# Cross-attention on one Trainium2 core: scores in three PSUM banks instead of two, and the turning and placing of the row maxima one slot later each

## The reference

```
q = x @ Wq + 2 * (x @ Aq @ Bq)          # 256 x 1024
k = c @ Wk + 2 * (c @ Ak @ Bk)          # 256 x 256
v = c @ Wv + 2 * (c @ Av @ Bv)
scores = q_head @ k_head.T / sqrt(32)   # per head 256 x 256
attn   = softmax(scores)
out    = x + context @ Wo + 2 * (context @ Ao @ Bo)
```

## Time and profile before

| | |
|---|---|
| time, median of 3 runs | 685.08 us (685.04, 685.08, 685.62) |
| the profiled execution's own time | 685.43 us |
| its span, first to last instruction | 683.2 us |
| busy: PE, PEld, DVE, ACT, POOL | 666.6, 527.1, 518.6, 468.5, 368.4 us |
| mean granted TensorE clock | 0.997 |
| attention loop, first to last scores (L1490) | 45.4 to 525.0 us |

### The profile page before, as it was taken

The page is one execution under the profiler, slowest core; times in us unless marked ns, Lnnn a source line. Parts: engine busy times, 40 slices in busy tenths (PEclk is TensorE's granted clock), DMA queues, the critical chain, the costliest instruction groups (busy, mean ns, idle before and its releaser), DMA issues.

```text
span 683.2 us, 14789 instructions
## 1 busy us (share of the span) xinstructions
PE 666.6 (98%) x4220; PEld 527.1 (77%) x4220; DVE 518.6 (76%) x1173; ACT 468.5 (69%) x1462; POOL 368.4 (54%) x316
## 2 busy tenths in 40 slices
PE   8999999999999999999999999999899999999998
PEld 6797777877877787787788778777676788888886
DVE  4768888787787778778777877878887898855542
ACT  5657888888888888888888888887678443222220
POOL 3548634852772484376258437625867005876732
PEclk9999999999999999999999999999999999999999
DMA  8957665674676567466656756657567244655331
GB/s 275 342 178 194 199 191 157 198 205 133 178 209 190 161 194 208 154 172 191 184 163 195 205 172 169 189 185 215 183 209 226 90 138 155 215 185 185 123 119 66
DMA packets 103797, 124.67 MB, mean 182 GB/s; under 512 B 9280, under 2 KB 85312, under 8 KB 103760
## 3 DMA queue, kind: packets, MB, share of 16 engines
q1 hardware_dynamic: 103760, 124.23, 59.9%
HBM read 86.18 MB, written 38.01 MB: 182 GB/s over the span
## 4 chain that ended last, share of the span: by engine, by line
PE 62%; DVE 20%; ACT 9%; issue 6%; DMA 2%; DVEq 0%; ACTq 0%; POOL 0%; SPq 0%; POOLq 0%
PE banks L1665 17%; PE banks L1472 12%; DVE neg_max L1128 7%; PE banks L1490 7%; PE banks L1531 6%; PE banks L1470 6%; PE banks L1520 5%; ACT banks L897 5%; PE banks L1507 5%; DVE turned_sb L1149 4%; PE banks L1451 2%; DVE x_both L1169 2%; ACT probs_t L908 2%; DVE q_stage L1120 2%; DVE max_parts L1137 1%
## 5 line engine op out<-in xcount | busy, mean ns | idle before, releaser
L897 ACT ACTIVATE banks<-banks,neg_max 128x256 f32<-128x256 f32 x512 | 230.3, 453 | 37.5 <-DVE neg_max L1128 32.9
L781 POOL TENSOR_TENSOR q_stack<-turned_sb,head_mask 8x512 fp32r<-8x512 f32 x128 | 138.6, 1083 | 189.2 <-DVE turned_sb L1149 183.0
L1128 DVE TENSOR_REDUCE neg_max<-banks 128x2 f32<-128x512 f32 x256 | 174.8, 686 | 34.3 <-PE banks L1490 32.1
L908 ACT ACTIVATE probs_t<-banks 128x512 f32<-128x512 f32 x256 | 155.1, 606 | 47.2 <-PE banks L1507 46.5
L1472 PE MATMUL banks<-x_both,w_hi 128*128 128x512 f32 x448 | 162.5, 395 | 0.0
L1470 PE MATMUL banks<-x_both,w_lo 128*128 128x256 f32 x448 | 118.4, 280 | 0.0
L1490 PE MATMUL banks<-k_stack,q_stack 96*128 96x256 f32 x512 | 113.7, 304 | 4.2 <-ACT banks L897 3.4
L1490 PEld LDWEIGHTS banks<-k_stack,q_stack 96*128 96x128 f32 x512 | 79.8, 190 | 45.2 <-issue 20.2
L897 ACT ACTIVATION_READ_ACCUMULATOR banks<-banks,neg_max 128x1 f32 x512 | 107.4, 210 | 0.0
L1507 PE MATMUL banks<-q_stack,k_stack 104*128 104x512 f32 x256 | 102.0, 399 | 0.0
L1470 PEld LDWEIGHTS banks<-x_both,w_lo 128*128 128x128 f32 x448 | 84.6, 189 | 9.2
(11 more groups left out here) (156 smaller groups left out, 1150.1 us busy)
## 6 DMA issues: line engine op xcount, KB each, us to landing
q_stack<-q_parts SPq DMA_DIRECT2D x192, 128.0 KB, 3.0
q_parts<-q_stage SPq DMA_DIRECT2D x64, 256.0 KB, 3.7
raw<-ct SPq DMA_DIRECT2D x32, 256.0 KB, 3.8
raw<-xt SPq DMA_DIRECT2D x32, 256.0 KB, 3.9
scales<-r_rows SPq DMA_DIRECT2D x64, 128.0 KB
context<-ctx_stage SPq DMA_DIRECT2D x64, 128.0 KB, 3.8
stage<-xn SPq DMA_DIRECT2D x16, 512.0 KB, 5.1
w_hi<-context SPq DMA_DIRECT2D x14, 512.0 KB, 6.9
```

Of the source, the lines that this page charges most:

```text
L781: nc.gpsimd.tensor_tensor(q_stack[rows, u % RING, heads], turned_sb[rows, u % 2].unsqueeze(1).broadcast_to([M_ROWS, 2, S]), head_mask[rows ...
L897: last = nc.scalar.activation(score_bank[c % 2][:, S * h:S * (h + 1)], score_bank[c % 2][:, S * h:S * (h + 1)], ACT.Exp, bias=neg_max[:, u ...
L908: nc.scalar.activation(probs_t[:, u % 2, t, 2 * hp:2 * hp + 2, :].rearrange("p a b -> p (a b)"), st_bank[j % 2], ACT.Exp, scale=-1.0).then ...
L1128: nc.vector.tensor_reduce(out=neg_max[:, u % 2, 2 * c:2 * c + 2], in_=score_bank[c % 2].rearrange("p (h t) -> p h t", h=2), axis=AXIS, op= ...
```

## The change

Scores go to PSUM banks 0, 1 and 5 in turn (bank 5 is not used in the loop before). By `score_bank(s)` the index within the batch picks the bank, with 30 and 31 in banks 0 and 1, so that each batch begins at bank 0; `bank_freed(s)` gives the number of finished exponentials that scores s wait for: those of the scores three before, of two before for the first two scores of a batch, of five before for the third. VectorE turns the maxima in the slot with c = 1, behind the maximum of that slot, instead of c = 0, where the split stays. GpSimd places in c = 2. Nothing else moves in the text.

```diff
-TURN = 1
+TURN = 2
...
-        score_bank = [banks[:, i, :] for i in range(2)]
+        score_banks = [banks[:, i, :] for i in (0, 1, 5)]
...
+        def score_bank(s):
+
+            return score_banks[s % SLOTS % 30 % 3]
+
+        def bank_freed(s):
+
+            i = s % SLOTS
+            return s - (2 if i < 2 else 5 if i == 2 else 3) + 1
...
                     last = nc.scalar.activation(
-                        score_bank[c % 2][:, S * h:S * (h + 1)], score_bank[c % 2][:, S * h:S * (h + 1)], ACT.Exp,
+                        score_bank(s)[:, S * h:S * (h + 1)], score_bank(s)[:, S * h:S * (h + 1)], ACT.Exp,
...
-                                        in_=score_bank[c % 2].rearrange("p (h t) -> p h t", h=2),
+                                        in_=score_bank(s).rearrange("p (h t) -> p h t", h=2),
...
                 if c == 0 and here:
                     split_max(b, u)
-                if c == 0 and u >= 0 and not (last and u > NG):
+                if c == 1 and u >= 0 and not (last and u > NG):
                     turn_max(b, u)
...
-                need(pe, exp_done, b * SLOTS + (s - 1))
+                need(pe, exp_done, b * SLOTS + bank_freed(s))
                 for h in range(2):
                     last = nc.tensor.matmul(
-                        score_bank[c % 2][:, S * h:S * (h + 1)],
+                        score_bank(s)[:, S * h:S * (h + 1)],
```

## The result

| | kernel before | kernel after |
|---|---|---|
| median, beside each other | 685.15 us (684.61 to 685.65, 12 runs) | 686.3 us (684.96 to 689.41, 12 runs) |
| ratio to before | | 1.0020, 95% interval 1.0012 to 1.0029 |
| the profiled execution and its span | 685.43, 683.2 us | 687.70, 685.9 us |
| first to last `scores_t` of the loop | 54.9 to 539.6 us | 55.8 to 541.7 us |

The change makes the kernel 0.2% slower where 1.2% faster was forecast. The profiled execution of after is 1.4 us above its own median, and its runs spread over 4.4 us where those of before spread over 1.0.

What follows compares the result with a forecast made beforehand. TensorE's own work was taken to bound the attention loop. First batch 2.2, six steady batches 5.4 (0.9 each) and last batch 0.5 sum to 8.1 us gained, giving 677.0 us for the median, range 672 to 682.

Steps and rivals of the forecast that it cites:

- The third bank: Steady batches: one more slot, 1.52 us, of slack ends the exponentials' waits at slots 18, 22 and 23, 1.0 us a batch.
- The turn: I take 0: VectorE, slots 4u + 1: the turn delays the projection split 0.5, with 0.3 left; cost 0, bounds 0 and 0.5, four times a batch.
- the fourth rival: Projection bank becomes the bound: TensorE stands 0.7 at slots 11, 19, 27 and 3; slower, 697.7 us; chance 0.09.
- The placement: I take 0: GpSimd (POOL): the later placement is ready 1.5 us before TensorE wants it in slot 4u + 4; cost 0.
- SyncE's queue: Rows, spread, q and stack keep their times while TensorE comes 1.0 earlier; cost 0.1 us a batch, bounds 0 and 0.6.
- the second rival: SyncE's chain takes it back, stack loads as late as TensorE is early; steady batch gains 0.4, 680 us; chance 0.15.
- The first batch: Of 5.0 us waits for exponentials, 2.2 go, the rest moves to projection banks VectorE frees no earlier; bounds 0.5 and 5.0.
- The last batch: High part of the weight is ready 1.0 earlier, given back in slots 4 to 20; gain 0.5 us, bounds -3 and +3.
- Slot 8 comes 0.7 later: Last batch: with the split of q 2.24 us behind slot 10's maximum, slot 8 comes 0.7 later, slot 20 about level.
- the wait in slot 25 shrinks by 1.0: Last batch from slot 20 on: no projection left to wait for, so the wait in slot 25 shrinks by 1.0 us.
- The clock: Last batch: one more half-clock stretch of 3.4 us would cost at most 1.7; taken as 0.
- The third rival: Two new half-clock stretches in the last batch, 3.4 us, leave 4.7 of 8.1; 680.4 us; chance 0.06.

Runs made afterwards that it cites:

- e9: e5 with turn and placement of group 5 one slot later outside the last batch; 678.05 us, ratio to before 0.9891.
- e10: e9 with turn and placement of group 2 in the first batch also one slot later; 677.18 us, ratio to before 0.9885.
- e2: Kernel before, two score banks, with turn in a group's second slot and placement in its third; 695.29 us, ratio to before 1.0142.
- e6: Three score banks, turn in a group's first slot as before, only the placement late, in its third; 683.96 us, ratio to before 0.9976.
- e1: Three score banks, with turn and placement where they were in the kernel before; 681.02 us, ratio to before 0.9939.
- e8: Kernel after with the placement in the group's second slot, right behind the late turn; 694.46 us, ratio to before 1.0132.
- e3: Kernel after with four entries of SyncE's list in steady batches reordered, input chunk 3 behind group 7's stack load; 681.39 us, ratio to before 0.9940.
- e5: e1 with the four entries of SyncE's list in the order of e3; 680.32 us, ratio to before 0.9920.
- e11: Kernel after, with group 4's turn and placement back in slots 16 and 17 outside the last batch; 681.05 us, profiled execution 678.00.
- e4: Kernel after, with turn and placement of the last batch as in the kernel before; 685.70 us, ratio to before 0.9999.
- e12_first_all_but_4: e10 with every turn and placement of the first batch but those of groups 4 and 8 one slot later; 677.01 us, ratio to before 0.9870.

## Why the prediction was wrong, point by point

**The third bank: right.** The waits at slots 18, 22 and 23 are gone, and with the list reordered and group 5's turn late a batch goes from 59.43 to 58.43 us (e9, e10), the 1.0 us that was worked out of the earlier trace rows. Alone the bank gives 0.6 of it and 0.6% in all.

**"The turn: I take 0": the term itself held, its surroundings did not.** In steady batches no projection bank was late for the turn in slots 11, 27 and 3; the fourth rival (697.7) did not come. But the turn, moved out of slot 16, let a split of x start while GpSimd's high parts ran. That the third bank covers the next maximum is right as well: with the move and two banks a batch takes 60.33 (e2).

**"The placement: I take 0": this step failed.** I asked who waits for the placement and found 1.5 us to spare, and of GpSimd's high parts of x I looked at those of slots 14 and 17, which "start earlier or as before". I did not ask what VectorE runs at the same moments, nor what becomes of the high parts of slots 15 and 16. Both missed something: the placement of group 4 held the split of x at 322.37 for 0.65 us, and that of group 3 put the high parts of slots 15 and 16 later, one of which held the split at 317.98 as long. The warning stood in the rows of the step: placements of 1.04 us with a longest of 1.55. Moved alone, the placement costs 0.6 us a batch (e6 against e1), as much as both moves together (59.39 against 58.84). What the late turn costs without the late placement is not shown: e8, made to tell, brought waits of its own.

**"SyncE's queue: 0.1 a batch, bounds 0 and 0.6": this term was mis-sized.** It measured 0.75 on average by reordering the list (e3), and 0.96 in the batch shown, so that a batch gains 0.05 of 1.0, and of the second rival's condition (stack loads land as late as TensorE is early) nearly all came true. With the turn left early it is 0.1 (e1 against e5), the size that I had; the late split of x makes the difference. I followed the chain of group 0 and looked only for the end of the turn in it. The load that became late first was that of group 7, and what held it in the list was the load of an input chunk, released by a split of x. e3 removes it by the list, and e11 by the split in the execution that was profiled. The second rival had 0.4 us a batch left and 680, because it knew only TensorE's earliness and not that the loads would go out later.

**The first batch: this term was mis-sized.** Start and first batch together end 0.15 later, where 2.2 were to be won. From `scores_t` to `scores_t` the batch went from 60.78 to 60.05, a gain of 0.7, but its first `scores_t` came 0.9 later (55.8 against 54.9), a point that lies between 53.8 and 56.2 in the kernels here. With the third bank alone the batch gained nothing (60.74 in e1): the 5.0 us of waits for exponentials are gone, and 3.0 us for splits of q, as the prediction said, and others took their place. The kernel after waits for stack loads instead; waits of PEld in the first batch, 45 to 116 us, e1_banks_only and then after:

```profile
PEld banks L1481 <- DVE q_stage L1131: 3.0, 4, 1.5
...
PEld banks L1499 <- DMA q_stack<-q_parts: 2.5, 3, 1.5
```

The profiled execution of e11 has a first batch of 58.66 us, 2.1 less than before and 1.4 less than after. It is the fastest of its kernel, so that the 2.2 can be had is a sign and not shown.

**The last batch: wrong in sign, right in mechanism.** "Slot 8 comes 0.7 later", the wait moving from the weight's high part to the split of q, is what the waits show (5.0 for 1.1, 3.4 for 4.8). The part from slot 20 on, where "the wait in slot 25 shrinks by 1.0", missed that in slots 28 to 32 VectorE's sums meet the placements, 1.7 us for two sums, and the scaling behind them frees the context's bank 1.3 late. Instead of 0.5 gained, the late turn costs 2.2 us from slot 16 of the seventh batch to the end, in profiled executions (e3 against e1, after against e4), and 1.4 by the medians of after and e4.

**The clock: taken as 0, it gave a little back.** In the last batch the granted clock stays at 1.00 in the kernel after and in all others here but e9. e9 has the half clock and e10 not, and their rests differ by 0.3, well inside the bound of 1.7. The third rival's new stretches did not come; the waits ahead of slots 8, 12 and 16 measured 1.3 us, where 1.5 to 1.9 were expected.

## What to carry to other kernels

When work is moved from one slot to another, list for its new time not only who waits for it but what the engine that it can hold up, or be held up by, is doing (here GpSimd and VectorE), and look for instructions whose longest time is well above their median: they may already meet something. Where one engine issues all transfers from a list, the slack of a load is that of the slowest entry ahead of it, so follow every entry's wait, not the one that the change touches. Two edits that each cover or spoil the other's slack should be run apart: here -5 and +10 us gave +1, and the better half with one turn of eight moved (two in the first batch) and four list entries reordered gives 1.15%.

## What the runs showed of the hardware

A conversion of 128 x 8 numbers on VectorE, 0.17 us in five of nine cases in 60 us of the kernel after, took 1.16 to 1.23 in three: each of the three began 0.08 to 0.16 us behind a subtraction of 1.28 on GpSimd. A 128 x 512 subtraction of 0.69 took 1.33 to 1.41 beside GpSimd's instructions. When VectorE's instruction started 0.05 us earlier than GpSimd's, it kept its 0.69, and GpSimd's two took 2.66 instead of 2.15. In one case 0.05 us, in another 0.08, decided which of the two was held.

One execution of e12_first_all_but_4 took 2189.5 us with a granted clock of 1.0 from start to end. Its matmuls of 512 columns took 2.9 times as long as the same ones of e10_turns_2_5 (first row of each: x448, min, median, max in ns), while VectorE's busy time stayed at 520 us:

```profile
L1481 PE MATMUL banks<-x_both,w_hi x448: 999/1152/1157, 164.8 to 1514.3; 128*128 128x512 f32 x150
```

```profile
L1481 PE MATMUL banks<-x_both,w_hi x448: 389/396/501, 52.9 to 453.5; 128*128 128x512 f32 x150
```

The profile gives no cause for that, and none is offered.
